# Attention by pairs of query tiles, values by channel, and a reordered head

## What is computed

```python
x = x + minGRU(layernorm(x))             # gates x @ Wz, x @ Wh, forward and backward, scan over time, @ W_out
q = layernorm(x) @ Wq.T; k = ctx @ Wk.T; v = ctx @ Wv.T      # ctx: 4 x 1601 x 256
x = x + softmax(q @ k.T / 16) @ v
x = x + FFN(layernorm(x))                # product keys: batch norm, top-k of two key halves, experts down and up
```

## Time and profile before

| what | value |
|---|---|
| time, median of 3 runs | 415.46 us |
| the profiled execution's own time | 416.85 us |
| its span, first to last instruction | 415.1 us |
| PE busy | 397.8 us (96%) |
| DVE, ACT, POOL busy | 72%, 59%, 52% |
| recurrence, attention, FFN (PE starts) | to 97, to 296, to 415 us |

### The profile page before, as it was taken

The page is one execution under the profiler, slowest core; times in us unless marked ns, Lnnn a source line. Parts: engine busy times, 40 slices in busy tenths (PEclk is TensorE's granted clock), DMA queues, the critical chain, the costliest instruction groups (busy, mean ns, idle before and its releaser), DMA issues. The chain is left out here.

```text
span 415.1 us, 7901 instructions
## 1 busy us (share of the span) xinstructions
PE 397.8 (96%) x2582; PEld 367.0 (88%) x2582; DVE 297.7 (72%) x1104; ACT 245.7 (59%) x539; POOL 215.9 (52%) x208
## 2 busy tenths in 40 slices
PE   2999999999999999999999999999999999999877
PEld 1788888899899999999999999999778998999766
DVE  4889777786366676457565555565695999799996
ACT  3687759354465655456573534443566887779462
POOL 2588999764263224334333212000147767989994
PEclk9999999999999999999999999999999998999999
DMA  7800223003422222231232100000100000000101
GB/s 223 299 0 3 76 56 101 8 7 127 109 64 64 55 81 77 59 80 52 58 98 59 54 2 2 0 2 0 28 1 2 0 3 1 27 28 26 41 25 65
DMA packets 19993, 21.38 MB, mean 52 GB/s; under 512 B 3181, under 2 KB 16625, under 8 KB 19953
## 3 DMA queue, kind: packets, MB, share of 16 engines
q1 hardware_dynamic: 18832, 19.96, 16.4%
q10 hardware_dynamic: 1120, 0.92, 0.8%
HBM read 18.78 MB, written 2.10 MB: 50 GB/s over the span
## 5 line engine op out<-in xcount | busy, mean ns | idle before, releaser
L847 DVE TENSOR_TENSOR att_pTl<-context_pR,att_pTh 128x512 fp32r<-128x512 f32 x64 | 37.4, 586 | 26.4 <-ACT att_pTh L759 26.1
L1191 POOL TENSOR_TENSOR ffn_prod<-ffn_first,ffn_near 128x1024 f32<-128x1024 f32 (+1 forms) x29 | 54.1, 1882 | 2.1 <-DVE ffn_first L1608 2.1
L866 DVE TENSOR_REDUCE att_mx<-keep_pQ 128x1 f32<-128x402 f32 x64 | 35.3, 567 | 24.2 <-PE keep_pQ L77 24.2
L759 ACT ACTIVATE att_pTh<-context_pR 128x512 fp32r<-128x512 f32 x64 | 32.4, 516 | 9.8 <-PE context_pR L1018 9.0
L1762 PE MATMUL ffn_pT<-keep_ident,ffn_prod 128*128 128x128 f32 x240 | 29.5, 277 | 4.3 <-POOL ffn_prod L1191 4.3
L1762 PEld LDWEIGHTS ffn_pT<-keep_ident,ffn_prod 128*128 128x128 f32 x240 | 27.3, 143 | 6.5 <-DVE ffn_hT L1641 4.8
L223 POOL TENSOR_TENSOR gru_z<-gru_z,gru_g 128x512 f32<-128x512 f32 x16 | 28.8, 1801 | 8.0 <-DVE gru_g L428 8.0
L1018 PE MATMUL context_pR<-keep_ident,att_prob 128*128 128x128 f32 (+1 forms) x208 | 32.8, 272 | 0.0
L984 PE MATMUL context_pA<-context_cNh,att_pTh 128*128 128x256 f32 (+1 forms) x104 | 31.4, 301 | 0.8 <-DVE att_pTl L847 0.8
L984 PE MATMUL context_pA<-att_cNh,att_pTh 128*128 128x256 f32 (+1 forms) x104 | 31.1, 299 | 0.0
L759 ACT ACTIVATE att_vTh<-context_pR 128x256 fp32r<-128x256 f32 x16 | 6.1, 384 | 39.3 <-PE context_pR L1023 39.3
(11 more groups left out here) (332 smaller groups left out, 1307.9 us busy)
## 6 DMA issues: line engine op xcount, KB each, us to landing
keep_raw<-in_ctxT SPq DMA_DIRECT2D x24, 256.0 KB, 2.6
keep_raw<-in_ctx SPq DMA_DIRECT2D x24, 256.0 KB, 2.7
out<-keep_x SPq DMA_DIRECT2D x16, 128.0 KB, 1.7
keep_x<-in_x SPq DMA_DIRECT2D x3, 512.0 KB, 9.9
gru_wout<-in_W_out SPq DMA_DIRECT2D x1, 512.0 KB, 8.4
keep_raw<-in_fWq SPq DMA_DIRECT2D x2, 256.0 KB
keep_raw<-in_ctxT SPq DMA_DIRECT2D x8, 32.5 KB, 3.8
keep_raw<-in_ctx SPq DMA_DIRECT2D x4, 65.0 KB
```

Of the source, the lines that this page charges most:

```text
L759: act.activation(to, bank, ACT.Copy).then_inc(bank_high, 1)
L847: dve.tensor_tensor(to, bank, half(it, 0, n)[0].bitcast(F32), ALU.subtract).then_inc(bank_free, 1)
L866: last = dve.tensor_reduce(mx[:, h, j:j + 1], pS[:, j, 0:min(SPANS[j][1], CTX) - SPANS[j][0]], AX.X, ALU.max)
L1191: return eng.tensor_tensor(prod[:, i % PB, a:b].rearrange("p h (i j) -> p h i j", j=KEYS), (factor if factor is not None else first[:, n % ...
```

## The change

1. Attention goes by pairs of tiles. `pTh` and `pTl` hold two tiles side by side (256 columns). The value product takes the context as stationary and the probabilities of both tiles as moving operand, A for channels 0 to 127 and B for 128 to 255, each in 39 matmuls of 256 columns into one half of `pA`. Its result is the transposed value, so `val`, its copies and the V transposes go; V is now one ACT copy and one DVE subtraction of 128 x 512 a pair, straight from `pA` to `vTh`, `vTl`. The scale 1/rowsum moves into the addition to x (a `scalar_tensor_tensor`).
2. There are two kinds of slots. Even: scores, with O of two tiles after the second bank and P0, P1 after the third, then P2, E, S, A0, P3, A1, A2, A3 (X between the last three). Odd: scores, then B0, E, P0, B1, P1, B2, P2, B3, V, P3 (Q ahead of P0 and P1). Slot 1 has its P and Q and no A. There are three more slots behind the 16th; the last has O of tiles 14 and 15 and F2, F3.
3. ACT rounds the context pieces of slots 0 to 2 at the slot's end, those of later slots ahead of everything else in it.
4. The FFN's query weights and `down` are laid over the first context half's memory; their loads and pieces wait for the scores of tile 11. The FFN stage reserves that memory.
5. In the head PE runs 13 products of the identity with itself before the first transposes and 4 behind them, into a bank that nothing reads. ACT calls a sigmoid on one column at its start, rounds only the first weight ahead of `xTh` and the other three behind it; DVE makes `nbias` and `bias_half` behind `xTl`. Products 1, 4 and 5 take their `wl` part last and wait for it there. The copies of batch 1's `xT` and one batch's normalisation stand at other units.

```diff
-        for m in range(2):
+        act.wait_ge(mhalf_set, 1)
+        act.activation(nmean[:, 0:1], mhalf[:], ACT.Sigmoid).then_inc(table_set, 1)
+
+        def weight_high(m):
             act.wait_ge(ld_w[m], 16)
             act.activation(wh[:, m], w[:, m], ACT.Copy).then_inc(wh_ready, 1)
 
...
+        weight_high(0)
         for k in range(DC):
             act.wait_ge(x0T_mm, k + 1)
             act.activation(xTh[:, 0, k], pT[:, k], ACT.Copy).then_inc(x0Th_ready, 1)
-        for m in range(2, 4):
-            act.wait_ge(ld_w[m], 16)
-            act.activation(wh[:, m], w[:, m], ACT.Copy).then_inc(wh_ready, 1)
+        for m in range(1, 4):
+            weight_high(m)
...
+                if n == 2:
+                    high(1)
...
+            if b == 2:
+                dve.wait_ge(table_set, 1)
...
-        dve.wait_ge(ld_bias, 16)
-        dve.tensor_scalar(nbias[:], bias[:], -1.0, None, ALU.mult).then_inc(nbias_ready, 1)
-        dve.tensor_scalar(bias_half[:], bias[:], 0.5, None, ALU.add).then_inc(half_ready, 1)
         for k in range(DC):
             dve.wait_ge(x0Th_ready, k + 1)
             dve.tensor_tensor(xTl[:, 0, k], pT[:, k], xTh[:, 0, k].bitcast(F32), ALU.subtract)\
                 .then_inc(x0Tl_ready, 1)
+        dve.wait_ge(ld_bias, 16)
+        dve.tensor_scalar(nbias[:], bias[:], -1.0, None, ALU.mult).then_inc(nbias_ready, 1)
+        dve.tensor_scalar(bias_half[:], bias[:], 0.5, None, ALU.add).then_inc(half_ready, 1)
...
+        def dense(count):
+
+            for _ in range(count):
+                pe.matmul(pP[:, 3, 0:P], ident[:], ident[:], start=True, stop=True)
+
         pe.wait_ge(ident_ready, 1)
+        dense(DENSE)
         first_transposes()
+        dense(UNITS)
...
-                if n == 1:
-                    pe.wait_ge(wl_pool, 1)
-                if n == 2 * DC:
-                    pe.wait_ge(wl_pool, 2)
-                    pe.wait_ge(wl_dve, 2)
                 cols = slice(ch * P, (ch + 1) * P)
+                if n in (1, 2 * DC, 2 * DC + 1):
+                    pe.wait_ge(wh_ready, 2 * way + m + 1)
+                    for i, part in enumerate(((wh, xTh), (wh, xTl), (wl, xTh))):
+                        if i == 2 and m == 1:
+                            pe.wait_ge(wl_pool, way + 1)
+                        if i == 2 and m == 0:
+                            pe.wait_ge(wl_dve, way + 1)
+                        for k in range(DC):
+                            last = pe.matmul(pP[:, n % 4], part[0][:, 2 * way + m, k, cols], part[1][:, 0, k],
+                                             start=(i == 0 and k == 0), stop=(i == 2 and k == DC - 1))
+                    last.then_inc(proj_mm, 1)
+                    if n == 2 * DC:
+                        transposes(1)
+                        attention_weights()
+                    continue
...
-                if n == UNITS:
-                    attention_weights()
...
-    ORDER = "V P0 P1 E O P2 S A0 P3 A1 A2 A3"
+    PAIRS = TILES // 2
+    EVEN = "O-4 O-3 P0-1 P1-1 P2-1 E S-4 S-3 A0-2 P3-1 A1-2 A2-2 A3-2"
+    ODD = "B0-3 E P0-1 B1-3 P1-1 B2-3 P2-1 B3-3 V-3 P3-1"
 
...
+        if g == 0:
+            out += [("X", 1, 0), ("X", 1, 1)]
+        if g == 1:
+            out = [("P", 0, 0), ("P", 0, 1), ("P", 0, 2), ("E", 1, 0), ("Q", 1, 0), ("P", 0, 3), ("Q", 1, 1)]
+        b = (g + 2) // TPB
+        if 2 <= b <= BATCH + 1 and (g + 2) % TPB == 0 and g < TILES or g == TILES:
+            b = BATCH + 1 if g == TILES else b
+            out.insert(out.index(("A", g - 2, 2)), ("X", b, 0))
+            out.insert(out.index(("A", g - 2, 3)), ("X", b, 1))
+        b = (g + 1) // TPB
+        if 2 <= b < BATCH and (g + 1) % TPB == 0:
+            out.insert(out.index(("P", g - 1, 0)), ("Q", b, 0))
+            out.insert(out.index(("P", g - 1, 1)), ("Q", b, 1))
         if g == TILES:
-            out.insert(out.index(("P", TILES - 1, 3)), ("X", BATCH, 0))
-            out.insert(out.index(("A", TILES - 1, 1)), ("X", BATCH, 1))
+            rest = [it for it in out if it[0] not in "EO"]
+            out = rest[:2] + [("O", g - 4, 0), ("O", g - 3, 0)] + rest[2:]
         if g == TILES + 1:
-            v, o, s = out
-            out = [("F", 0, 0), v, ("F", 0, 1), ("X", BATCH + 1, 0), o, ("X", BATCH + 1, 1), s, ("F", 0, 2), ("F", 0, 3)]
+            out = [it for it in out if it[0] in "BV"] + [("F", 0, 0), ("F", 0, 1)]
+        if g == TILES + 2:
+            out = [("O", g - 4, 0), ("O", g - 3, 0), ("S", g - 4, 0), ("S", g - 3, 0), ("F", 0, 2), ("F", 0, 3)]
         return out
...
+    EARLY = {"O": (2, 2), "P": (3, 2)}
 
...
+        if g >= TILES or g % 2 and g > 1:
+            return []
+        if g == 1:
+            return {2: [("P", 0, 0)], 3: [("P", 0, 1)]}.get(j, [])
+        return [it for it in SLOTS[g] if it[0] in EARLY and EARLY[it[0]][0] == j and it[2] < EARLY[it[0]][1]]
...
+    pT = [st.sb(n, [P, CT, 2 * P], F32R) for n in ("pTh", "pTl")]
+    vT = [st.sb(n, [P, DC, 2 * P], F32R) for n in ("vTh", "vTl")]
...
+        if b == BATCH:
+            eng.wait_ge(score_mm, KB * TPB * (BATCH - 1))
...
-        elif kind == "P" and a >= 1:
-            eng.wait_ge(value_mm, NG * (a - 1) + i + 1)
-        elif kind == "V" and a >= 2:
-            eng.wait_ge(bank_full, place[("O", a - 2, 0)] + 1)
+        elif kind == "P" and a >= 2:
+            eng.wait_ge(value_mm, NG * (a // 2 * 2 - 1) + i + 1)
...
+        sp.wait_ge(score_mm, KB * TPB * (BATCH - 1))
         sp.dma_start(keep["down"][:], d["downT"].rearrange("(k p) n -> p k n", p=P)).then_inc(ld_key, 16)
...
+        def values_high(p):
+
+            act.wait_ge(value_mm, 2 * NG * (p + 1))
+            if p >= 1:
+                act.wait_ge(bank_full, place[("O", 2 * p - 1, 0)] + 1)
+            act.activation(vT[0][:].rearrange("p c n -> p (c n)"), pA[:], ACT.Copy).then_inc(value_high, 1)
...
+        for g in range(TILES + 3):
+            if 2 < g < TILES:
+                for i in pieces_at(g):
...
+                elif it[0] == "V":
+                    values_high(it[1] // 2)
...
+            if g <= 2:
+                for i in pieces_at(g):
+                    piece_high(i)
...
+            dve.scalar_tensor_tensor(out=x_all[:, g], in0=pR[:, n % RING, 0:D], scalar=rinv[:, g % TPB:g % TPB + 1],
+                                     in1=x_all[:, g], op0=ALU.mult, op1=ALU.add).then_inc(bank_free, 1)
...
+            dve.wait_ge(value_high, p + 1)
+            if p >= 1:
+                dve.wait_ge(bank_full, place[("O", 2 * p - 1, 0)] + 1)
+            to, hi = (v[:].rearrange("p c n -> p (c n)") for v in (vT[1], vT[0]))
+            dve.tensor_tensor(to, pA[:], hi.bitcast(F32), ALU.subtract).then_inc(value_low, 1)
...
-            if kind == "A":
-                pe.wait_ge(bank_free, place[("P", a, i)] + 1)
-                if i == 0 and a >= 1:
-                    pe.wait_ge(val_ready, a)
-                if i == 0 and a == 0:
-                    pe.wait_ge(gru["x2_ready"], 2 * BATCH)
-                    pe.wait_ge(gru["piece_lo"], PIECES)
+            if kind in "AB":
+                p, ch = a // 2, "AB".index(kind)
+                if kind == "A":
+                    pe.wait_ge(bank_free, place[("P", a + 1, i)] + 1)
+                    if i == 0 and p >= 1:
+                        pe.wait_ge(value_low, p)
+                    if i == 0 and p == 0:
+                        pe.wait_ge(gru["x2_ready"], 2 * BATCH)
+                        pe.wait_ge(gru["piece_lo"], PIECES)
                 for kt in GROUPS[i]:
                     rows, par = (CLAST if kt == CT - 1 else P), (a // TPB) % 2
-                    l = [p[0:rows, kt] for p in pT]
-                    r = [c[par][0:rows, kt] for c in (cNh, cNl)]
-                    pe.matmul(pA[:, 0:D], l[0], r[0], start=(kt == 0), stop=False)
-                    pe.matmul(pA[:, 0:D], l[0], r[1], start=False, stop=False)
-                    last = pe.matmul(pA[:, 0:D], l[1], r[0], start=False, stop=(kt == CT - 1))
+                    out = pA[:, ch * 2 * P:(ch + 1) * 2 * P]
+                    l = [c[par][0:rows, kt, ch * P:(ch + 1) * P] for c in (cNh, cNl)]
+                    r = [t[0:rows, kt] for t in pT]
+                    pe.matmul(out, l[0], r[0], start=(kt == 0), stop=False)
+                    pe.matmul(out, l[0], r[1], start=False, stop=False)
+                    last = pe.matmul(out, l[1], r[0], start=False, stop=(kt == CT - 1))
...
-            elif kind == "V":
-                pe.wait_ge(val_ready, a + 1)
-                for k in range(DC):
-                    last = pe.transpose(bank[:, k * P:(k + 1) * P], val[:, a % 2, k * P:(k + 1) * P], ident[:])
             else:
-                pe.wait_ge(bank_free, place[("V", a, 0)] + 1)
+                pe.wait_ge(value_low, a // 2 + 1)
+                cols = slice(a % 2 * P, (a % 2 + 1) * P)
                 last = split_products(pe, bank[:, 0:D], [
...
+        with ExitStack() as late:
```

(4 more changed lines are left out.)

117 lines of the change are left out of this document (47 added, 70 removed).

## The result

The changed kernel takes 409.7 us (median of 6 runs, 409.19 to 411.48); the kernel before, run beside it, 416.48. The ratio is 0.9846 [0.9817, 0.9875], so the change is faster by 1.5%, and the forecast of 408.4 is 1.3 us from it. Of these 1.3, 0.8 is in the spans, where 7.1 us were forecast and 6.3 measured. The profiled execution of the changed kernel took 410.63 us, its span 408.7. The other 0.5 comes of the step from a profiled execution to a median: I took 1.4 between them, as in the three runs before (416.85 and 415.46), and here it is 0.9 (410.63 and 409.7).

A forecast was written before the change was run, and what follows sets the result against it. PE's list of instructions plus its waits was taken to bound the kernel. Attention 5.7 and head 1.4 us make 7.1, taking the profiled 416.85 to 409.75; less 1.4 to the median gives 408.4, range 404.5 to 412.0.

The forecast's parts named there:

- The bank waits: Attention, PE waiting for a bank between A1 and A2: 8 of 16 such waits go, 0.8 us won.
- The turned product: Attention, value product with probabilities as moving operand: same 0.12 us each, so 0 in all, 3 us either way.
- The switches: Attention, first product after a transpose 0.08 us dearer: 0.6 us won in pairs, 0.3 lost by X transposes.
- I let all of it go: Attention, two waits of A for `pTl` and the weight loads they expose: all gone, 1.2 us won.
- small new waits: Attention, 0.4 us charged, bounds 0 to 2.5 (an exponential never late; one of each pair late by 0.3).
- Slot 16: End of attention: old waits for `val` and `vTl` go, 1.3 us won; O's new chain costs 1.0.
- ACT in time: Attention, exponentials done before the next scores: slack 1.8 us in even slots, 3.3 in odd; slot 3 1.3 late.
- The head: Before attention: unread products bring the clock's rise forward, batch 1's transposes then wait for `xn` until 17.8; 1.4 us won.
- A: Head: the clock does not rise in time or falls again; head wins 0.2 us, 409.6 in all; chance 0.12.
- B: Attention: new waits of 0.8 us in each of 7 pairs eat 5.6 us, 414.0 in all; chance 0.12.
- C: Attention: context pieces ahead of the exponentials on ACT delay scores, PE loses 12 us, 420.4 in all; chance 0.04.
- D: Attention: value product 0.005 us cheaper each (3 us), no new waits (0.4 us), 405.0 in all; chance 0.12.

The follow-up runs named there:

- head alone: The kernel before with only the changed head (every edit of `stage_gru`): 415.33 us, 0.9983 of the kernel before.
- attention alone: The changed kernel with `stage_gru` of the kernel before: 410.2 us, 0.9846 of the kernel before.
- the experiment: The changed kernel with DVE's moments of batch 3 and POOL's root one slot later: 408.54 us, 0.979 of the kernel before; attention 1.42 us less.
- pieces ahead in 4th slots: The changed kernel with context pieces behind the slot's items, except ahead in slots 3, 7, 11, 15: 410.96 us, 0.9871 of the kernel before.

## Why the prediction was right, and where it was not

**What bounds the kernel**: right. PE's list and waits set the time; DVE at 10.23 of 11.85 us in an even slot, more than I had supposed, cost nothing in a plain pair.

**The pair** was forecast at 11.9 + 10.4 = 22.3 and took 22.18. In the table of a pair, three terms make up the 0.77. Four transposes at 0.109 are 0.44, as forecast (3.5 in all).

The bank waits were mis-sized. In the kernel before, all 16 tiles have the step of 0.22 between A1 and A2, and in the changed kernel none has it: 27 value products took 3.39 before, from the first of A1 to the scores, and take 3.24 now in the A half as well. I had excused only the B items. That is 0.21 a pair, 1.7 us in all, 0.9 more than the term. DVE's row of before shows what PE waited for there, the low part of P2, done at 155.71, while A2 began at 155.77:

```profile
155.02 0.69 DVE L847 TENSOR_TENSOR att_pTl<-context_pR,att_pTh 128x512 fp32r<-128x512 f32 x1 [1.50 <-ACT att_pTh L759]
```

ACT copied this P2 behind the exponentials. In the even slot after, P2 stands ahead of them, its low part is done at 136.15, and A2 begins at 137.44.

The turned product is a little cheaper. In a stream of value products the mean step is 0.1179 us before and 0.1163 after (0.1180 in "head alone", 0.1163 in "attention alone"), so it goes with the turned product. That is 0.12 a pair and 1.0 us for the 624, a third of the 3 us that I held open. What in the operands makes the difference, no run shows.

The switches were counted twice. Behind a run of transposes the first product takes 0.20 instead of 0.12, but the last transpose takes 0.03 instead of 0.109, so the two cancel: four transposes take 0.35, and with the 0.08 behind them that is 4 x 0.109. Once a transpose is priced at 0.11, a switch adds nothing, and the 0.6 won and 0.3 lost for switches should both have been 0.

**"I let all of it go"**, the waits for `pTl`, was the step that failed in attention. Slot 1 has no A, as I said, but slot 2 kept a wait, and it costs 1.42 us by the experiment, more than both waits of before by my price (1.2; their steps exceed the usual by 0.78 and 0.38). I had asked which PE work stands ahead of A, and not what stands ahead of P0's subtraction on DVE. The "small new waits" of 0.4, in turn, were not there: no exponential came late.

**Slot 16** was forecast at 1.0 for `vTl`. It costs 1.3, in two parts. The first is a wait of 0.5 on a ring bank (`pTl`, P2's subtraction), which I had not counted: ACT and DVE serve P2 and V in one queue, and I had counted V's chain alone. The second is the wait for `vTl` itself: it is done at 270.07, and O starts at 270.31, 0.40 behind the last transpose where 0.03 is usual.

**ACT in time**: right. In slot 3, where I had put the exponentials 1.3 us late, they were 0.1 late (122.68 against 122.57). The alternatives show how narrow it is: 5.1 us lost one slot earlier, 20.7 at the other end.

**The head**: the mechanism at the transposes was right in each link (a rise before 10 us, PE done with product 4 near 16.3, then held by `xn` at 17.8; measured 16.47 and 17.44). Two numbers in it were not. An fp32 product of 128 columns is two instructions (26 for the 13) of 0.21 us each, so the 13 took 5.53 us and ended at 7.05. That is near the later of my two ends (7.7), not the nearer (4.5), and it cost nothing only because PE has no other work before 7.06. And "from 20 us on PE is the bound, so this passes through" failed: 1.77 us became 0.58. A stretch in which PE is busy 77.00 of 77.00 shows no slack on PE, but it doesn't show how much slack the others have. DVE's `hT` was ready 0.55 us before PE came for it, and a PE that came 1.7 us earlier met it. The trace of before had this number (33.06 and 33.61), and I didn't look for it.

The Trainium skill (GPSIMD Engine Reference, "Specifications") has VectorE and GpSimd in contention for certain DVE forms. The rows here are narrower than my reading of it. `xTl` took 1.28 with its last 0.27 beside `wl`, and 1.29 with `nbias` ahead of it. The four subtractions of 512 columns into `pTl` that have POOL beside them for nine tenths of their time take 0.69 us in the mean, and so do the 37 without it. But `nbias` of 8 columns took 1.13 instead of 0.17.

**The rivals.** A is refuted by the cadence at 9.88, and by the kernel without unread products. B has its kind of wait in slots 2 and 16, not in seven pairs. C's mechanism is shown, but not in this order of work. D came in part: no small waits (0.4), and a cheaper product (1.0 of its 3).

**The sum.** For attention, 3.5 (transposes) + 0 (switches) + 1.7 (banks) + 1.0 (cadence) + 1.3 - 1.3 (the two tails) + 1.2 - 1.4 (`pTl`) gives 6.0, and 6.07 was measured. The forecast of 5.7 is close to it by luck: 0.9 too little for banks, 1.0 for the cadence and 0.4 charged for small waits stand against 0.3 too much for switches, 0.3 too little charged in slot 16 and 1.4 in slot 2. In the whole, 0.8 too much for the head and 0.4 too little for attention partly cancel, and 0.3 us more came in the FFN, for the reason in the last section.

**What stays open.** Kernels with the same head reach tile 0 up to 0.5 us apart, the turned product is cheaper for a reason that no run shows, and the dip in the FFN comes and goes.

## What to carry to other kernels

A microsecond won early on the bounding engine is only worth what the next producer's lead allows: ask of the first product behind it how long its operand had been ready, since a full busy column doesn't tell. When an order of work is changed, follow each engine's queue ahead of the operation that the bounding engine waits for; both surplus waits that went away here came from operations of DVE without hurry that stood ahead of an urgent one and could be moved by one step. Price an instruction by the whole run from start to start, so that a cheap last step and a dear first one aren't counted apart. And keep tiny VectorE operations of the kinds below clear of long GpSimd ones.

## What the runs showed of the hardware

**Tiny DVE operations beside POOL.** In the changed kernel, `nbias` (8 columns) takes 1.13 us, a sum of two single columns 1.08, and each 0.15 to 0.17 elsewhere. Thirteen such operations ahead of the FFN take 1.05 to 1.32 us, among them 9 of the 16 sums (`rowsum`), and each of them ends within 0.04 us of the end of a POOL operation that it overlaps. The seven sums without POOL beside them take 0.15. Not every tiny operation suffers: the 16 reciprocals of one column, most of them beside POOL, all take 0.16 to 0.17.

**The clock's rise and fall.** With `stage_gru` of before, the 0.23 cadence began at 15.07 in one kernel and at 13.38 in another with the same head ("attention alone"). The Trainium skill (TensorE: Matmul & The Clock Gate, "What's actually happening") has the throttled level as the default, released by activity; that work brings the rise forward is shown (before 9.88 with the unread products). A pause of 4.67 us cost 2.2 us more than itself, one of 4.65 us cost 1.5 more.

**A dip in the FFN that comes and goes.** In the changed kernel the granted clock fell to 0.50 in the FFN, though PE was busy throughout, ahead of the dip and in it:

```profile
332.00:334.00 2.00, 2.00 (x11) 2.00 (x11) 0.63 (x7) 0.60 (x4) 0.00 (x0) 0.50 0.00 0
```

The dip lasts from some 330.8 to 337.6 us. In the earlier trace rows a shorter one begins near 349.6, behind small waits of PE. What it costs depends on where it lies. Of the fourteen profiles, four have none, and their rest is 114.6 to 114.7. Two have one of some 3 us that begins 42 us behind the FFN's first product ("head alone", "pieces ahead in 4th slots"), and their rest is hardly longer, 114.7 to 114.8. Three have one of some 3 us that begins 53 us behind it ("before" among them): 115.95 to 116.01. Five have one of some 7 us that begins 41 to 42 us behind it: 116.2 to 116.3. This 1.5 us changes sides between kernels with the same FFN, and it is as large as some of the effects studied here. Why the dip comes in one profile and not in another, no run shows.
